# Patch embedding, attention and channel mixing on one core: embedded rows in PSUM, squares halved on GpSimd, a separate buffer for the normalised rows, and a new order of the work

## The reference

```python
# x (64, 3, 224, 224), txt (64, 77, 256)
h = layernorm(patches(x)) @ W + b          # 196 patches of 768 values per image -> 256
h = layernorm(h) * ln2_g + ln2_b
h = concat([h, txt], axis=1)               # (64, 273, 256)
h = h + attention(layernorm(h))            # within one token: 16 heads of 16; see below
h = h + ffn(layernorm(h))
# ffn: x_prev is the row before (zeros for the first)
#   xr = mu_r*x + (1-mu_r)*x_prev ; xk = mu_k*x + (1-mu_k)*x_prev
#   out = sigmoid(xr @ W_r.T) * (relu(xk @ W_k.T)**2 @ W_v.T)
```

## Time and profile before

| | |
|---|---|
| median of 3 runs (lowest, highest) | 1633.04 us (1625.81, 1639.91) |
| the profiled execution: its time, its span | 1637.46 us, 1635.7 us |
| mean granted TensorE clock | 0.968 |
| TensorE matmul / weight load busy | 89% / 85% of the span |
| VectorE, ScalarE, GpSimd busy | 81%, 67%, 60% |
| DMA | 227.65 MB, mean 139 GB/s; 617,470 of 702,658 packets under 512 B |

### The profile page before, as it was taken

One profiled execution on the slowest core, in us unless ns is written; L12 is line 12 of the kernel. 1 busy time (PEld: TensorE's weight loads), 2 busy tenths in 40 slices (PEclk: granted clock), 3 DMA queues, 4 the chain that ended last, 5 costly groups with the idle time before them and its releaser, 6 DMA issues. The chain is left out here.

```text
span 1635.7 us, 53680 instructions
## 1 busy us (share of the span) xinstructions
PE 1454.6 (89%) x18762; PEld 1382.2 (85%) x18762; DVE 1332.3 (81%) x3075; ACT 1099.9 (67%) x2230; POOL 973.6 (60%) x1507
## 2 busy tenths in 40 slices
PE   4678899899999999999999999999999999998856
PEld 4677898898998898889898898998988988897756
DVE  5576888798988989898898888898898988888642
ACT  4455777677777776776777676777777776775543
POOL 2121566567656666666766765675675676576556
PEclk8798999999999999999999999999999999999988
DMA  4279979889877887888887896898898799887651
GB/s 121 59 141 138 141 147 150 125 159 157 143 157 141 147 155 143 150 137 165 149 140 157 151 141 127 167 157 141 152 154 140 151 159 140 156 151 118 131 74 37
DMA packets 702658, 227.65 MB, mean 139 GB/s; under 512 B 617470, under 2 KB 673854, under 8 KB 702394
## 3 DMA queue, kind: packets, MB, share of 16 engines
q1 hardware_dynamic: 702394, 224.23, 77.9%
HBM read 121.64 MB, written 89.64 MB: 129 GB/s over the span
## 5 line engine op out<-in xcount | busy, mean ns | idle before, releaser
L1026 PE MATMUL bank<-wqkv,xnT 128*126 128x384 f32 (+1 forms) x1728 | 354.2, 349 | 5.5 <-issue 5.5
L1118 PE MATMUL bank<-wtok,xT 128*98 128x258 f32 x2304 | 310.2, 290 | 12.0 <-DVE xT L770 11.4
L1026 PEld LDWEIGHTS bank<-wqkv,xnT 128*126 128x126 f32 (+1 forms) x1728 | 294.0, 185 | 18.3 <-issue 10.2
L1118 PEld LDWEIGHTS bank<-wtok,xT 128*98 128x98 f32 x2304 | 294.2, 171 | 14.6 <-DVE xT L770 13.2
L667 POOL TENSOR_TENSOR mixp<-mixf,mixp 128x364 fp32r<-128x364 f32 x192 | 185.2, 976 | 107.2 <-ACT mixp L1000 106.6
L921 ACT ACTIVATE arena<-qk,ymask 128x768 f32<-128x768 f32 x192 | 164.0, 926 | 97.6 <-DMA qk<-qkv_dram 97.6
L843 DVE TENSOR_TENSOR qkvt<-bank,bqkv 126x384 f32<-126x384 f32 (+1 forms) x288 | 154.0, 548 | 48.5 <-PE bank L1026 47.0
L654 POOL TENSOR_TENSOR dT<-zT 128x364 f32<-128x364 f32 x96 | 79.7, 851 | 153.9 <-ACT zT L994 153.9
L609 POOL TENSOR_TENSOR rs<-ve,small 126x3 f32<-126x3 f32 (+1 forms) x160 | 150.3, 940 | 12.5
L607 POOL TENSOR_TENSOR ve<-mv,small 126x3 f32<-126x3 f32 (+1 forms) x160 | 58.8, 368 | 158.8 <-DVE mv L865 104.0
L765 DVE TENSOR_REDUCE xs<-xim 84x14 f32<-84x1792 f32 x64 | 128.7, 2011 | 23.1 <-ACT xim L955 22.8
(11 more groups left out here) (121 smaller groups left out, 3339.6 us busy)
## 6 DMA issues: line engine op xcount, KB each, us to landing
xim<-in_x SPq DMA_DIRECT2D x128, 294.0 KB
qk<-qkv_dram SPq DMA_DIRECT2D x48, 768.0 KB, 8.3
qkv_dram<-qkvt SPq DMA_DIRECT2D x96, 378.0 KB
arena<-qkv_dram SPq DMA_DIRECT2D x384, 48.0 KB, 3.9
qkv_dram<-qkvt SPq DMA_DIRECT2D x48, 336.0 KB
o_dram<-probs SPq DMA_DIRECT2D x288, 48.0 KB, 1.9
out<-h SPq DMA_DIRECT2D x96, 126.0 KB
on<-o_dram SPq DMA_DIRECT2D x64, 126.0 KB
```

What stands on the lines that cost most here:

```text
L1026: ins = mm(psum, left(a, k), right(b, k), start=t == 0, stop=t == len(terms) - 1)
L1118: ins = mm(place("tok", c)[0:PT, 0:E + 2], xT[:, a, i0:i0 + GRID // 2, :].rearrange("p i w -> p (i w)"), wtok[:, b, ch, :], start=t == 0, ...
```

## The change

1. `y` moves from SBUF to PSUM bank 7, which no TensorE job writes any more; TensorE jobs share the other seven. yn writes it there, and st2, hg and h read it there. `sel` gets a small tile of its own, and `turn` becomes a function that VectorE calls too.
2. ScalarE squares `xcols` in place. GpSimd adds the two halves of each 128 squares (new operation `sqh`, 84x896), and VectorE's ssq sums 64 instead of 128 values per group. So the next load waits only for xcols, while the next xcols waits for ssq; and sq now waits for the transposes x.
3. `z` gets its own tile beside `on`. o_in no longer waits for zt, and z no longer for ont.
4. mix takes `z` from zt's bank instead of `z_prev` from `zT`, with `mu - 1` as factor (one GpSimd instruction at the start makes it), so L661's memset goes, and zt's bank is held until mix 3 or 4 instead of until ztc.
5. The tables `AT` and `BANK` are new.

```diff
-AT = dict(load=[0], xcols=[1345, 1388, 1607], sq=[2596], ssq=[2858], ...
+AT = dict(load=[0], xcols=[1669, 1697, 1955], sq=[3210], ssq=[3957], ... sqh=[3563])
-BANK = dict(x=[5, 7, 2], tok=[7, 2], stat=[5], xt=[6, 5], qkv=[4, 1, 6, 3, 4, 3], s=[0, 1], pt=[1, 4], av=[1, 6],
-    ont=[1, 3], wo=[3, 6, 5], zt=[1, 6], k=[4, 0], r=[3, 6, 4], val=[0, 1, 3])
+BANK = dict(x=[5, 3, 1], tok=[3, 1], stat=[5], yn=[7], xt=[5, 6], qkv=[2, 0, 4, 0, 5, 2], s=[6, 2], pt=[2, 6],
+    av=[2, 6], ont=[2, 4], wo=[4, 6, 0], zt=[4, 6], k=[0, 0], r=[0, 2, 0], val=[5, 0, 2])
...
-        y = sb("y", [PT, 2, E])
-        sel = y[:, 0, 0:2 * GRID].rearrange("p (a w) -> p a w", w=GRID)
+        sel = sb("sel", [PT, 2, GRID])[:, :, :]
...
-        z = on
+        z = sb("z", [TT, TILES, E])
...
-                    ont=(on_lo, [1, 2]), wo=(h2_sb, [1, 2, 3]), zt=(zT_sb, [1, 2]), k=(kr_sb, [1, 2]),
+                    ont=(on_lo, [1, 2]), wo=(h2_sb, [1, 2, 3]), zt=(mix_sb, [3, 4]), k=(kr_sb, [1, 2]),
...
-                            after(x_stats, q, k - 1, 1)
+                            after(x_cols, q, k - 1, 3)
...
-                        after(z_pe, q, k - 1, 2)
                         after(on_pe, q, k - 1, 2)
...
+                    for k in due(q, s, "sqh", 0):
+                        x_sq.wait(pool, q, k, 1)
+                        halves = xcols[:, :].rearrange("p (w a q) -> p a w q", a=2, q=64)
+                        x_half.done(P.tensor_tensor(halves[:, 0, :, :], halves[:, 0, :, :], halves[:, 1, :, :], ALU.add))
...
-                        edge_sb.done(P.memset(zT[:, :, b], 0.0))
...
-                        x_stats.done(V.tensor_reduce(xs[:, :], xim[:, :].rearrange("p (w q) -> p w q", q=128), AX.X, ALU.add))
+                        x_stats.done(V.tensor_reduce(xs[:, :], xcols[:, :].rearrange("p (w q) -> p w q", q=128)[:, :, 0:64], AX.X, ALU.add))
...
+                    y = place("yn", 0)[0:PT, 0:2 * E].rearrange("p (c e) -> p c e", c=2)
...
                             mix_sb.done(V.scalar_tensor_tensor(out=mixf[:, kk, :], in0=dT[:, kk, :], scalar=mus[:, w, kk:kk + 1],
-                                                               in1=zT[:, kk, 0:CT], op0=ALU.mult, op1=ALU.add))
+                                                               in1=place("zt", kk)[:, 0:CT], op0=ALU.mult, op1=ALU.add))
...
-                                x_tr.wait(act, q, k - 1, 3)
-                                x_sq.wait(act, q, k - 1, 1)
+                                x_stats.wait(act, q, k - 1, 1)
...
+                        x_tr.wait(act, q, k, 3)
                         x_cols.wait(act, q, k, 3)
-                        x_sq.done(A.activation(xim[:, :], xcols[:, :], ACT.Square))
+                        x_sq.done(A.activation(xcols[:, :], xcols[:, :], ACT.Square))
...
-                            on_pe.wait(act, q, k, 2)
                             z_pe.wait(act, q, k - 1, 2)
```

More of the change, by code:

```diff
@@ L52 @@
 SLOT, IMG, QUAD = 4000, 3000, 12000
[L53 to L67, removed]
@@ L69 @@
-BANK = dict(x=[5, 7, 2], tok=[7, 2], stat=[5], xt=[6, 5], qkv=[4, 1, 6, 3, 4, 3], s=[0, 1], pt=[1, 4], av=[1, 6],
-    ont=[1, 3], wo=[3, 6, 5], zt=[1, 6], k=[4, 0], r=[3, 6, 4], val=[0, 1, 3])
-PE_ORDER = ("s", "pt", "av", "x", "tok", "stat", "xt", "qkv", "ont", "wo", "zt", "k", "r", "val")
+AT = dict(load=[0], xcols=[1669, 1697, 1955], sq=[3210], ssq=[3957], sqm=[3700, 4470], x=[2181, 2230, 2294],
+    xh=[2185, 2665, 2793], xl=[2447, 2936, 2938], tok=[3284, 4235], stat=[4349], statc=[4502], statr=[4564],
+    rstd1=[4751], txt=[10039], yn=[4994, 5027], st2=[5363, 6176], mv2=[6258, 6408], rstd2=[7003], hg=[6499, 6546],
+    h=[7422, 7424], hdma=[7972], st3=[11152, 11153, 11181], mv3=[11159, 11381, 11415], rstd3=[11590], xn=[12365,
+    12369, 12451], xt=[12776, 12913], xnh=[13021, 13090], xnl=[13045, 13352], hb=[17897], qkv=[13478, 13620, 13859,
+    14545, 14778, 14868], qb=[13853, 13888, 14473, 14584, 15128, 15134], qkv_out=[15069, 15102, 15251],
+    qk_in=[15990], v_in=[17700], qplace=[17642, 17844], kspread=[17503, 17554, 17579, 17601], s=[17867, 17883],
+    mx=[18038, 18071], sub=[18076, 18110], exp=[18254, 18334], pt=[18328, 18472], ptc=[18414, 18517, 18540, 18577],
+    av=[18588, 18715], rec=[18712, 18782], osb=[18749, 18907], o_out=[19180], o_in=[23964], ont=[24924, 25001],
+    onh=[25031, 25075], onl=[25228, 25310], wo=[25423, 25462, 26182], h2=[25571, 25648, 26186], st4=[25711, 25812,
+    26390], mv4=[26387, 26401, 26423], rstd4=[26582], z=[26677, 26682, 26761], zt=[26891, 26972], carry=[26015],
+    ztc=[26989, 27059], d=[27242, 27295], edge=[27535], mix=[27577, 27597, 28660, 28695], mixh=[27923, 28007, 29409,
+    30069], mixl=[28197, 28199, 30406, 30996], k=[28671, 29065], kr=[28992, 29134], ksq=[29673, 30168], kah=[30110,
+    30608], kal=[31077, 31239], r=[31117, 31534, 31752], rt=[31454, 31880, 31887], val=[31880, 32100, 32405],
+    rv=[31960, 32132, 32743], add=[33340, 33476, 33994], out=[33582, 33624, 35930], sqh=[3563])
@@ L1027, in product @@
                 return ins
-            def turn(q, s, kind, j):
-                same = [job for job in JOBS if BANK[job[2]][job[3]] == BANK[kind][j]]
-                at = next(i for i, job in enumerate(same) if job[0] == s and job[2] == kind and job[3] == j)
-                for back in range(1, 8 * len(same)):
-                    wrap, i = divmod(at - back, len(same))
-                    _, _, other, jj, k = same[i]
-                    k += wrap * COUNT[other]
-                    if exists(q, k, COUNT[other]):
-                        signal, steps = READ[other]
-                        return signal.wait(pe, q, k, steps[jj])
             pe.wait_ge(prep_pool, 26)
```

68 lines of the change are left out of this document (42 added, 26 removed).

## The result

The changed kernel takes 1686.68 us (median of 4 runs, 1677.71 to 1698.34) against 1634.47 us for the kernel before in the same session: a ratio of 1.033, 95% interval 1.0235 to 1.0422. It is 3.3% slower. The forecast was 1607 us, the range ended at 1649, and slower by over 1% had a chance of 0.14: the prediction was wrong in sign and outside its range. The profiled execution took 1698.34 us, the longest of the four, with a span of 1696.5 us and a mean granted TensorE clock of 0.943 (0.968 before).

A forecast was written before the change was run, and what follows sets the result against it. TensorE was taken as the bound, busy 87.93 of 94 us per quad. Terms of -2.0 us per quad over about 13.6 quads (-27), -5 start and +2 end took 1637.46 to 1607 us; own range 1592 to 1624, 8-in-10 range 1577 to 1649.

The forecast's parts named there:

- y in PSUM: On VectorE, hg reading y from PSUM falls from 908 to about 475 ns, 55 us of VectorE; 0.7 us saved per quad.
- SyncE's order: Reordered DMA issues on SyncE shorten TensorE's waits at ont and s: 1.6 and 0.9 us saved per quad in two thirds.
- load third: Third of a quad with the image load; moving it from before o_in and qk_in saves 1.6 of 2.4 us, bounds 0 and 2.4.
- patch third: Third of a quad with the patch copies; o_in goes ahead of them, 3.6 us earlier, saving 0.9 us of the 1.32 at ont.
- L800's hold: VectorE's L800 is held up while GpSimd runs; without that, TensorE's wait at wo goes, 0.7 us saved per quad.
- Patch third, s: TensorE's wait at the scores stays, as qk_in still stands behind the patch copies: 1 to 2 us left, nothing gained.
- The addition: GpSimd's new addition of halves takes 2.15 us (1.8 to 2.6) and makes k wait for mixl, 0.7 us more per quad.
- Banks: TensorE's jobs have seven PSUM banks instead of eight: 0.5 us more per quad, bounds 0 and 3.
- The start: At the kernel's start, an earlier load and a shorter ssq save 5 us, bounds 0 and 16.
- The end: The latency chain at the kernel's end, with adds a little later, costs 2 us, bounds -2 and 5.
- The price for reading PSUM: By the skill's rule, 576 VectorE operations reading PSUM cost 65 ns more each, 37 us; the forecast sum left it out.
- GpSimd becomes the pacer: Rival, chance 0.16: GpSimd, given 8.6 us more per quad, comes late in all three thirds, by 1.3 us each; about 1655 us.

The follow-up runs named there:

- unheld copy: The changed kernel with VectorE's two copies of q written as a sum over an axis of length one: 1634.39 us, ratio 1.0006.
- The addition taken away: The changed kernel without GpSimd's sqh, VectorE summing all 1792 squares again: 1649.95 us, ratio 1.0112.

## Why the prediction was wrong

**The step that failed** is in "y in PSUM". I had found the right mechanism: L800, with all tensors in SBUF, is held up while GpSimd runs. Then I applied it only to the operations that leave it (hg, h, mix: "by the same mechanism they can only lose stalls") and not to the one that stays, qplace. I had drawn the kind too narrowly: L800 reads two tensors from SBUF and the copy reads one, and it is held all the same (541 to 4276 ns). The kernel before already showed it as exposed: median 557 ns, mean 630, highest 1205. And the new order puts hb, the second add and the addition of halves around it. The sum had no term for the copies. Measured, they cost VectorE 97 us more, and 52 us of time against the same kernel with an unheld copy: that is 3.8 us per quad in the prediction's own count of 13.6, against a forecast gain of 2.0. This is the whole loss, but not the whole miss: with the copies unheld the time is 1634 us and not 1607. The other 27 us lie mainly in a second step that failed, the terms for SyncE's order. The sum took 1.6 us per quad as saved in the load third and 0.9 in the patch third; the run with the unheld copy shows the waits moved and not gone. ont went from 25.3 to 6.7 us and wo from 11.1 to none, but s went from 28.2 to 53.1 us, and av, which the sum didn't have, from 0.4 to 21.1.

**The waits, term by term.** hg's single line in the changed kernel answers to L800 in the earlier trace rows:

```profile
L818 DVE SCALAR_TENSOR_TENSOR bank<-bank,mv,g2b x128: 457/481/494, 38.5 to 1554.8; 98x256 f32<-98x256 f32 x128
```

- L800's hold, -0.7 per quad: right. The successor never passes 494 ns (h, L824, never 487), and the wait of wo for onl is gone. But the freed time was mostly taken by the copies: 61.3 (hg) + 20.3 (mix) + 13.6 (h) + 59.8 (ssq) = 155 us off, 97.4 on, 58 us less. All of VectorE's groups by line together fell by 58 us too; the page has 28.1 us less, as instructions that overlap count once there.
- Load third, -1.6, and patch third, -0.9: the wait at ont went as said, from 25.3 us to 0.7 us in the same stretch. The gain at s did not come: I took 1.6 of the 2.4 us at ont and s together as saved, and the copies put 2.5 to 4.2 us in place of the 0.96 at s.
- Patch third, s: "the wait at s there stays, since qk_in still stands behind the copies". Right that it stays, wrong in size: the prediction had 1 to 2 us of it. In the changed kernel it was 4.2 to 4.3 us in each quad, in 12 of 13 by the copies. With the hold removed the waits at s in all thirds were still 33.7 + 19.2 us over the steady part, up to 4.8 us at once, and moving qk_in ahead in this third gave 17 us.
- The addition: predicted 2.15 us, measured 2.117. That it makes k wait for mixl, +0.7 per quad: not seen in the steady part, no such row among the first waits. It cost about 37 us in "The addition taken away", where TensorE's wait for the copies fell by 49 us with it.
- ssq: predicted 1.05, measured 1.08 us. Right.
- Banks, +0.5: no wait is seen that would surely be theirs; no run gives the eighth bank back.
- The start, -5: the first scores come at 101.4 us and not 104.6, so -3. The end, +2: 67.6 us from the last scores to the end of the span against 67.8, so nothing.
- The price for reading PSUM by the Trainium skill ("VectorE: DVE Perf Modes", section on the TRN2 errata), an estimate of 65 ns more each: not in these rows. hg has a median of 481 ns against 476, mix from the bank 587 against 593.

**The rivals.** "GpSimd becomes the pacer" named the right engine and sign, but by another way, so its nearer number (about 1655 us) is luck: TensorE's waits don't name GpSimd, since the profile puts them down to the VectorE copy that GpSimd held. Of the signs listed for "wrong", the new wait of av for v came true (14.0 us). Most of the signs for "right" that could be read from one line each came true (hg, wo, ont, ssq, the addition), while the total missed: no sign was listed for the operation that I hadn't costed.

**With the hold gone and q ahead**, the changed kernel comes to 1617 us, inside the first range (1592 to 1624). That doesn't bear the forecast out: it takes a further change of order, which the prediction didn't have, and is 0.9% under the kernel before, where the forecast was 1.6% below its median. In the order as given, the PSUM move, the addition, z apart and the new order of SyncE together gave nothing (1634.39 us, ratio 1.0006) once the hold was gone.

## What to carry to other kernels

When a trace shows that an operation is held up by another engine, list every operation of that kind, and above all those that stay: a mean above the median (13% here) and a highest of twice the median mark them in the trace before. Then look at what the new order puts beside each. An operation that is hidden beside another engine's work cost nothing here until it outlasted that work, so compare the two durations, and try the form that can't be held, even if it takes 1.7 times as long.
